# Operand sums on another engine, reordered steps, and split weights kept off chip in a three-stage transformer kernel

## The reference

```python
y = clip((x * styles) @ weight.T * dcoefs + bias)          # conditioned projection
h = rms_norm(y); gate = gelu(h @ Wg.T + bg); hs = h @ Wh.T + bh
r, i = sigmoid(h @ Wr.T + br), sigmoid(h @ Wi.T + bi)
a = exp(-8 * softplus(alpha) * r)
out = scan(o = a * o + sqrt(1 - a * a) * hs * i)           # over the sequence
hs2 = out * gate + y
h2 = rms_norm(hs2)
g2 = gelu(h2 @ mlp_gate_w.T + mlp_gate_b)                  # 512 -> 1536
f2 = h2 @ mlp_fc_w.T + mlp_fc_b                            # 512 -> 1536
x1 = x + (f2 * g2) @ out_w.T + out_b + hs2                 # 1536 -> 512
# third part: conditioned norms of x1, a 3072 -> 512 -> 512 MLP, an int8-quantised product, added to x1
```

## Time and profile before

| | |
|---|---|
| median of the runs | 1802.99 us |
| the profiled execution | 1807.12 us, its span 1805.0 us |
| TensorE busy | 1754.0 us (97%) |
| VectorE, ScalarE, GpSimd busy | 1191.8, 891.6, 833.2 us |
| scan half, about | 0 to 463 us |
| gate and fc stage, about | 463 to 957 us |
| output stage, about | 957 to 1264 us |
| third part | to 1805 us |

### The profile page before, as it was taken

How to read it: one execution, slowest core, us unless ns; L and a number is a source line. 1 busy time by engine, 2 the same in 40 slices (tenths; PEclk the granted TensorE clock), 3 DMA queues, 4 the chain that set the end, 5 groups by cost and what they waited for, 6 DMA issues and landing times.

```text
span 1805.0 us, 23628 instructions
## 1 busy us (share of the span) xinstructions
PE 1754.0 (97%) x8039; PEld 1424.1 (79%) x8047; DVE 1191.8 (66%) x1737; ACT 891.6 (49%) x1325; POOL 833.2 (46%) x718
## 2 busy tenths in 40 slices
PE   9999999999789999999999999898999999999998
PEld 7888888887578787887887888776888888888886
DVE  8766676659769779677564334445986776686555
ACT  7655555655456565565562222223554453544533
POOL 1112222123667667667660000014577777877743
PEclk9999999999889999999999999999999999999999
DMA  5011110010232433332445657786744345444411
GB/s 201 1 47 47 47 46 19 28 70 27 82 126 94 148 110 109 117 124 70 170 145 198 208 185 232 260 297 227 258 130 164 118 141 182 119 156 149 136 40 59
DMA packets 105789, 229.63 MB, mean 127 GB/s; under 512 B 9906, under 2 KB 10162, under 8 KB 105700
## 3 DMA queue, kind: packets, MB, share of 16 engines
q1 hardware_dynamic: 75540, 152.97, 24.9%
q0 software_dynamic: 11776, 41.95, 7.0%
q10 hardware_dynamic: 18384, 33.56, 5.7%
HBM read 169.73 MB, written 58.72 MB: 127 GB/s over the span
## 4 chain that ended last, share of the span: by engine, by line
PE 83%; DVE 7%; DMA 3%; issue 3%; ACT 2%; POOL 1%; SPq 1%; DVEq 0%; ACTq 0%; POOLq 0%
PE bank L1031 22%; PE bank L342 16%; PE bank L1967 13%; PE bank L1093 12%; PE bank L2012 5%; PE bank L1991 4%; PE bank L322 4%; PE bank L1933 2%; PE bank L1942 2%; DVE h_parts L1435 1%; DMA raw_w<-int_W 1%; DVE mlp_w L1444 1%; PE bank L1103 1%; SPq L1860 1%; DMA raw_mlp_w<-mlp_gate_g 0%
## 5 line engine op out<-in xcount | busy, mean ns | idle before, releaser
L1031 PE MATMUL bank<-h_parts,mlp_w 128*128 128x512 f32 x2016 | 467.8, 394 | 25.4 <-DVE mlp_w L1439 9.7
L1031 PEld LDWEIGHTS bank<-h_parts,mlp_w 128*128 128x128 f32 x2016 | 382.6, 190 | 110.0 <-DVE mlp_w L1439 11.8
L342 PE MATMUL bank<-h_parts,gate_w 128*128 128x512 f32 x1536 | 351.4, 389 | 1.8 <-ACT gelu_out L532 1.3
L342 PEld LDWEIGHTS bank<-h_parts,gate_w 128*128 128x128 f32 x1536 | 288.1, 188 | 63.5 <-ACT gelu_out L532 1.7
L1093 PE MATMUL bank<-p_parts,mlp_out_w 128*128 128x512 f32 x1152 | 274.6, 395 | 12.2 <-DVE p_parts L1449 10.7
L1967 PE MATMUL bank<-operand_parts,int_w 128*128 128x512 f32 x1152 | 281.8, 394 | 0.6 <-DVE x_columns L1528 0.6
L1093 PEld LDWEIGHTS bank<-p_parts,mlp_out_w 128*128 128x128 f32 x1152 | 215.2, 189 | 62.9 <-issue 15.8
L1967 PEld LDWEIGHTS bank<-operand_parts,int_w 128*128 128x128 f32 x1152 | 213.1, 188 | 44.6 <-PE bank L1093 1.0
L594 POOL TENSOR_TENSOR decay_sq<-decay 128x512 f32<-128x512 f32 x32 | 38.3, 1196 | 274.5 <-DVE decay L680 274.5
L1362 POOL TENSOR_TENSOR product_out<-product_out,gelu 128x512 f32<-128x512 f32 x72 | 126.6, 1780 | 69.2 <-DVE product_out L1498 68.7
L1240 ACT ACTIVATE product_copy<-bank,vec_sb 128x512 f32<-128x512 f32 x144 | 98.9, 689 | 97.2 <-PE bank L1031 97.0
(11 more groups left out here) (306 smaller groups left out, 2850.7 us busy)
## 6 DMA issues: line engine op xcount, KB each, us to landing
p_d<-product_out SPq DMA_DIRECT2D x96, 256.0 KB, 2.1
p_tile<-p_d ACTq DMA_DIRECT2D x96, 256.0 KB, 4.3
raw_mlp_w<-mlp_gate_g SPq DMA_DIRECT2D x21, 512.0 KB, 3.8
raw_mlp_w<-mlp_fc_g SPq DMA_DIRECT2D x21, 512.0 KB, 4.5
xin<-xT SPq DMA_DIRECT2D x8, 1024.0 KB
hs_d<-u SPq DMA_DIRECT2D x8, 1024.0 KB, 5.0
hs_pair<-hs_d SPq DMA_DIRECT2D x8, 1024.0 KB, 5.4
x_columns<-xT SPq DMA_DIRECT2D x8, 1024.0 KB, 6.8
```

What stands on the lines that cost most here:

```text
L342: i = pe.matmul(bank[:], gw[:, w, s, k, m * P:(m + 1) * P], hr[:, q, t, k, :], start=k == 0 and n == 0, stop=k == KT - 1 and n == 2)
L1031: i = pe.matmul(bank[:], wb[g % 2][:, s, w, kk, :], hop[u % 2][o][:, t, kk, :], start=first and kk == 0 and n == 0, stop=kk == 1 and n == ...
```

## The change

1. Only visits 0 to 5 (the first pair, `NPREP` = 6) load raw weights, form sums and split. After the split SyncE stores the whole buffer to DRAM (`keep_parts`, 1.8 MB per k and chunk). The later visits with a new chunk (15, `RELOADS`) fetch the parts back in two pieces (`parts_back`): part 0 is what products 1, 5 and 6 read, part 1 the rest; the layout of `wb` is turned so that each piece is contiguous.
2. The sums of the operands (T1 to T4) move from GpSimd to VectorE. The steps beside the groups are spread anew.
3. At the seam to the gate and fc stage: mean-square steps earlier, the fc weights of visit 0, T4 and group 0's copies and sums moved into the last block of the scan half.
4. At the seam to the output stage: the first three tiles are split one step earlier.
5. In blocks 5 and 6 of the output stage: the small tables and four of the six slots are asked for ahead of the x1 stores and their waits.

```diff
-A11, A12, A22, S1, S2, S3, S4 = range(NM)
+A11, S1, S2, A12, S3, S4, A22 = range(NM)
+PARTS = ((0, A12), (A12, NM))
-NPREP = len(CHUNK)
+NPREP = FT // 2
+RELOADS = [v for v in range(NPREP, NV) if NEW[v]]
...  scan half, ScalarE, body (the early(-3) ahead of the block is gone)
+                if not nxt2:
+                    early(4 if not nxt else -3)        # after the square roots
                 for m in range(KT):
+                    if m == 2 and not nxt:
+                        early(5)                       # between the gelus
...  scan half, VectorE, body
+                if not nxt:
+                    early(4)                           # before the scans
+                if not nxt:
+                    early(5)                           # after the scans
...  SyncE
+        def keep_parts(k, n):
+            sp.wait_ge(w_lo[k], 2 * (n + 1))
+            sp.dma_start(w_d[2 * CHUNK[n] + k], wb[k][:]...).then_inc(w_stored[k], 16)
+
+        def parts_back(k, i, part):
+            a, b = PARTS[part]
+            sp.wait_ge(w_stored[k], 16 * NPREP)
+            sp.wait_ge(p_ps[(6, 4)[part]], 2 * (i - 1) + k + 1)
+            sp.dma_start(wb[k][:, a:b]..., w_d[2 * VISITS[i][2] + k, :, 4 * P * a:4 * P * b]).then_inc(w_back[k][part], 16)
         def visit(i):
             if i == 0:
+                keep_parts(0, 0)
                 next_pair(1)
-            n = PREP[i] + 1
-            ahead = NEW[i] and n < NPREP
-            if ahead:
-                sp.wait_ge(w_sum[0], 4 * n)
-                sp.wait_ge(w_lo[0], 2 * n - 1)
-                load_raw(0, n)
+            n = i + 1
+            if i < NPREP:
+                keep_parts(1, i)
+                if n < NPREP:
+                    sp.wait_ge(w_sum[0], 4 * n)
+                    sp.wait_ge(w_lo[0], 2 * n - 1)
+                    load_raw(0, n)
+            if i in RELOADS:
+                parts_back(1, i, 1)
             if i:
                 sp.wait_ge(p_end, i)
                 store(i - 1, 3)
-            if ahead:
+            if n < NPREP:
                 sp.wait_ge(w_sum[1], 4 * n)
                 sp.wait_ge(w_lo[1], 2 * n - 1)
                 load_raw(1, n)
+                keep_parts(0, n)
+            if n in RELOADS:
+                parts_back(0, n, 0)
+                parts_back(0, n, 1)
+                parts_back(1, n, 0)
...  SyncE, output stage, body
+            if b == LAST_FIRST:
+                last_small()
+            if b == NB - 2:
+                last_slots()                           # slots 2 to 5
             if b:
                 sp.wait_ge(r1, KT * b)
...
-                last_small()
...
             if b == NB - 2:
-                last_slots()
+                last_late_slots()                      # slots 0 and 1
...  TensorE, group: waits for w_lo in visits 0 to 5, for w_back in RELOADS
+            weights_ready(g, 0)                        # before product 1
+            weights_ready(g, 1)                        # before product 3
...  ScalarE
         def weights_high(k, n):
             act.wait_ge(raw_loaded[k], 16 * (n + 1))
             if n:
+                act.wait_ge(p_ps[4], 2 * (n - 1) + k + 1)
+                act.wait_ge(w_stored[k], 16 * n)
-            if g == NG - 1:
+            if g == NG - 2:
                 for n in range(HEAD):
                     tile_high(n)
             elif m == 3:
+                weights_high(0, 0)
                 operand_high(0, T3)
                 operand_high(0, T2)
-                weights_high(0, 0)
                 weight_sums_high(0, 0)
+            elif m == 4:
+                weights_high(1, 0)
+                weight_sums_high(1, 0)
+                operand_high(0, T4)
+                copy_1(0)
+                copy_5(0)
+            elif m == 5:
+                copy_6(0)
...  GpSimd: operand_sums and its calls are gone
...  VectorE
+        def operand_sums(u, part):
+            t = tsum[u % 2]
+            if part == 0:
+                dve.wait_ge(h_full, 2 * KT * (u + 1))
+                dve.tensor_tensor(t[T1][:], half(1, 0), half(0, 0), ALU.subtract).then_inc(t_sum, 1)
+                dve.tensor_tensor(t[T3][:], half(1, 1), half(1, 0), ALU.subtract).then_inc(t_sum, 1)
+            else:
+                dve.tensor_tensor(t[T2][:], t[T3][:], half(0, 0), ALU.add).then_inc(t_sum, 1)
+                dve.tensor_tensor(t[T4][:], half(0, 1), t[T2][:], ALU.subtract).then_inc(t_sum, 1)
...  beside, steps: 4 invert 0; 5 normalise 0; 6 invert 1; 7 normalise 1, low B11; 8 sums T1, T3, low B21;
...  9 sums T2, T4, low B22; 10 low T1, T3, T2; 11 low T4 (before: 5 to 8 invert and normalise in turn;
...  9 low B11, B21, B22; 10 low T1, T3; 11 low T2, T4)
+            if g == NG - 1:                            # before sum_out(g, ...)
+                for n in range(HEAD):
+                    tile_low(n)
         def early(m):
             elif m == 2:
-                for o in (B11, B21, B22, T1):
-                    operand_low(0, o)
+                operand_low(0, B11)
+                operand_low(0, B21)
+                operand_sums(0, 0)
+                operand_sums(0, 1)
             elif m == 3:
-                operand_low(0, T3)
-                operand_low(0, T2)
+                operand_low(0, B22)
                 weights_low(0, 0)
                 weight_sums_low(0, 0)
+                for o in (T1, T3, T2):
+                    operand_low(0, o)
+            elif m == 4:
+                weights_low(1, 0)
+                weight_sums_low(1, 0)
+                operand_low(0, T4)
+            elif m == 5:
+                for t in range(3):
+                    sum_out(0, t)
```

More of the change, by code:

```diff
@@ L823, in mlp_half, with own, summed @@
     rstd = [at(f"rstd2_{n}", [P, BT], where) for n, where in enumerate(ROOT_AT)]
-    wb = [at(f"mlp_w{k}", [P, 2, NM, 2, P], WB_AT[k], F32R) for k in range(2)]
+    wb = [at(f"mlp_w{k}", [P, NM, 2, 2, P], WB_AT[k], F32R) for k in range(2)]
+    def own(k, s):
+        return wb[k][:, A11:NM:3, s]
+    def summed(k, s):
+        return wb[k][:, S1:NM, s].rearrange("p (a b) k o -> p a b k o", b=3)[:, :, 0:2]
     raw = [at(f"raw_mlp_w{k}", [P, 4, 2, P], RAW_AT[k]) for k in range(2)]
@@ L847, in mlp_half @@
     w_lo = (early_sem("mlp_gate_low"), early_sem("mlp_fc_low"))
+    w_stored = (early_sem("mlp_gate_parts_stored"), early_sem("mlp_fc_parts_stored"))
+    w_back = [[early_sem(f"mlp_{n}_parts_back{part}") for part in range(2)] for n in ("gate", "fc")]
     ow = [at(f"mlp_out_w{n}", [P, 2, KT, D], where, F32R) for n, where in enumerate((G2, F2, O2))]
@@ L1038, in last_product, with weights_ready @@
             product(g, 4, X[g % 2], False)
+        def weights_ready(g, part):
+            k, i = g % 2, g // 2
+            if i < NPREP:
+                pe.wait_ge(w_lo[k], 2 * i + 1)
+            elif i in RELOADS:
+                pe.wait_ge(w_back[k][part], 16 * (RELOADS.index(i) + 1))
         def group(g):
             k, i = g % 2, g // 2
-            n = PREP[i]
-            pe.wait_ge(w_lo[k], 2 * n + 1)
+            weights_ready(g, 0)
             if g == 0:
@@ L1053, in group @@
             product(g, 1, X[k], True)
-            pe.wait_ge(w_lo[k], 2 * n + 2)
+            if i < NPREP:
+                pe.wait_ge(w_lo[k], 2 * i + 2)
             if g > 1:
@@ L1501, in group @@
             beside(g)
-            if g % 2 == 0 and g:
+            if g == NG - 1:
+                for n in range(HEAD):
+                    tile_low(n)
+            if g == 0:
+                return
+            if g % 2 == 0:
                 product_21(g // 2 - 1)
@@ L1510, in group @@
             sum_out(g, 2)
-            if g == 0:
-                operand_low(0, T4)
-            if g == NG - 1:
-                for n in range(HEAD):
-                    tile_low(n)
         def add_hs2(b, ks):
@@ L1544, in early @@
                 add_squares(0, 0)
+            elif m == -3:
+                add_squares(0, 1)
             elif m == -1:
-                add_squares(0, 1)
                 sum_low(0, 0)
@@ L1882, in run @@
                 sp.wait_ge(stored[t], 16 * NB)
-        return early_small, early_w1, early_c_rows, early_w2, early_slots, early, run
+        return early_small, early_w1, early_c_rows, early_w2, early_slots, late_slots, early, run
     def tensor_program(pe, mlp, bank_at):
```

169 lines of the change are left out of this document (83 added, 86 removed).

## The result

The changed kernel took 1818.26 us (median of four runs, 1817.50 to 1818.74) against 1804.11 (four runs, 1802.51 to 1806.01) of the kernel before on the same chip: ratio 1.0078, 95% interval 1.0060 to 1.0095. It is slower, by 14.1 us; 1814.3 was forecast. The profiled execution took 1818.66 us, its span 1816.9.

A forecast was written before the change was run, and what follows sets the result against it. TensorE was taken to bound the block-pair products, so only its holes could be won; +9.5 + 19 - 5.5 - 1.4 - 8.2 - 2.1 = +11.3 us on the median 1803.0 gave 1814.3 us, range 1782 to 1829.

The forecast's parts named there:

- The seam: From scan half to gate and fc stage: two 1.835 MB stores ahead of the raw weights delay TensorE, +9.5 us.
- The first visits: First six visits: raw gate loads wait behind fc split and store; losses 3.7, 3.7, 5.7, 7.2, taken as +19 us.
- Visits 6 to 23: Later gate and fc visits: nothing is split, so holes of pairs 2 and 3 go, -5.5 us; fetches cost nothing.
- a fetch that TensorE waits for: Sign of a wrong forecast, in the later visits; fetches 1 us late each visit would cost +15 us.
- The output stage: Low tiles split earlier -1.4 us, small tables asked for sooner -8.2, four slot loads moved ahead -2.1.
- the joint: Entry to the output stage: HEAD's low tiles ahead of the last sum remove the 1.43 us hole, -1.4 us.
- what is late next: Output stage, after the small tables come sooner: the x columns' load, for which VectorE waited 5.10 us without a hole.
- the next bound: Output stage: VectorE's mixed_w work, named with bounds of -5 to +5 us around the x1T store's count of nothing.
- the stores hide: Rival for seam and visits: loads behind the stores land as before; -24 us, 1779 us, chance 0.15.
- The slipping loop: Rival: GpSimd's multiply and SyncE's product stores pace the first visits (+27), with clock loss at holes; 1827 us, chance 0.17.
- Half hidden: Rival: seam as forecast, but the first visits lose only 1 to 2 us each, 6 in all; 1801 us, chance 0.17.

The follow-up runs named there:

- seam_early: The changed kernel with chunk 1's raw weights loaded and chunk 0's parts stored in the last scan block, ahead of the store of u; 1798.94 us.
- raw_first: The changed kernel with the raw gate load ahead of the store of the fc parts from visit 1 on, seam as it is; 1800.36 us.
- no_keep: The changed kernel without its stores and fetches of parts: all 21 chunks loaded raw and split; 1784.96 us.
- no_keep_gpsimd_sums: no_keep with the operand sums T1 to T4 back on GpSimd at the same steps; 1792.87 us.
- output_loads_only: The kernel before with only the change's order of small-table and slot loads in the output stage; 1798.25 us.
- both_orders: The changed kernel with the edits of seam_early and raw_first together; 1782.12 us.
- no_keep_early_2: no_keep with chunk 1's raw weights asked for in the last scan block, ahead of the store of u, run a second time; 1775.51 us.

## Why the prediction was right, and where it was not

**The seam: right in kind, the term too large.** Forecast +9.5, measured +4.8 with the start-up apart. One hole of over 20 us, ended by ScalarE's copy, stands where it was put, and TensorE returns 1.47 us after the landing (before 1.48). From the store of u to the landing it was 13.07 us before and is 20.84 now: the two stores cost 7.8 us, not 9.5. 3.67 MB at the 385 GB/s of this stretch are 9.5 us, but the queue before was not full all the time (321 GB/s from 487.58 to 500.65), and the stores took some of its empty room. The rest of the difference is the store of u, 3.0 us earlier by the scan half's own time, which the text had left in place "within 2 us either way". The Trainium skill (DMA: Bandwidth & Descriptors, Queues, rings and completion order) has each DMA engine consume a ring's descriptors in order; seam_early and raw_first agree, the place of the same transfers alone is worth 19.3 and 17.9 us.

The prediction left two holes of before out of its account (2.42 and 0.58). What it priced at nothing there, the earlier arrival of TensorE, proved so in the change: it arrived 9.3 us sooner (484.60 against 493.88) and only waited longer. But the move of the sums is worth 4.8 us at this point in no_keep against no_keep_gpsimd_sums, with both waiting 15 us for the DMA: it makes the store of u earlier, and through it all that stands behind it. The prediction looked only at TensorE's arrival.

**The first visits: right in all, not turn by turn.** Forecast 20.3, taken as 19, measured 20.9. From SyncE's release at 522.14 to the landing at 530.10 it was 8.0 us where 9.3 was worked out; from landing to product 5, 6.2 where 6.1 was. Of the terms, the four turns have holes of 2.57, 2.91, 5.49 and 4.49 us against 3.7, 3.7, 5.7 and 7.2. The 5.4 us that the holes do not explain lie in TensorE itself. Behind the hole of 4.23 us, 48 matmuls took 13.18 us, 2.3 more than at 0.2272 each, with the granted clock at 0.63 (third row of the stretches). The 72 at 559.35 took 1.1 more, the 36 at 595.45 took 0.7 more, and four other runs that end at a hole 0.3 each, as before (six in 1.66 instead of 1.36). For these visits the text had a clock loss only in one rival. It also had product 7 add nothing of its own, since it comes ready with product 5. Product 7's holes come first at each turn and make 9.55 of the 15.46 us; at the third turn, 581.01, product 7 waits 4.23 us and product 5 behind it not at all. All four turns lost less by holes than was worked out, and TensorE's slower runs filled the sum: that part is luck. That VectorE's later steps lengthen these turns was an estimate, and no run tests it.

**Visits 6 to 23: the size right, the reason wrong.** Forecast -5.5, measured -4.9 (less the 0.63 at 915.13, the late fetch behind the output weights: it had been placed 1 us before its need, and a fetch that TensorE waits for was named as a sign of being wrong, here a small one). But the reason given was that "nothing is split", and from it followed that the holes of group 11 stay; they fell from 2.86 to 0.43 us. no_keep splits everything and has none of these holes: the step that failed is the attribution. The new spread of the beside steps takes them away by itself, so they cannot be credited to the stores and fetches, which pay for nothing. That is why undoing them gains 33 us.

**The output stage: too hopeful.** Forecast -11.7 for its three parts, measured -7.8; the joint gave its 1.4. The four holes of before, 5.59, 2.10, 0.66 and 2.37 us, became 1.37, none, 1.05 and 2.13, and 0.81 and 0.16 are new: 5.2 us less. The clock loss of 2.6 behind the 5.59 went, and one of 1.4 came behind the 2.13 (12 matmuls in 4.38 us). TensorE waits for VectorE's p_parts each time, and at the first two VectorE itself had stood waiting for the load of the x columns:

```profile
1174.27 1.41 DVE L1586 SCALAR_TENSOR_TENSOR x_columns<-hs_odd,vec_sb,x_columns 128x512 f32<-128x512 f32 x2 [5.10 <-DMA x_columns<-xT]
1175.60 2.47 DVE L2629 BATCH_NORM_STATS2 stats<-x_tiles 128x6 f32<-128x512 f32 x4
...
1218.45 1.41 DVE L1586 SCALAR_TENSOR_TENSOR x_columns<-hs_even,vec_sb,x_columns 128x512 f32<-128x512 f32 x2 [10.65 <-DMA x_columns<-xT]
```

So "what is late next" was named rightly, the load of the x columns; that it makes no hole was the mistake. Ahead of 1179.57 the third part's statistics (2.47 us) stand behind the same wait of 5.10 that made no hole a block earlier. At the second, the wait of before was 6.96 (1203.19) and made no hole; the load is asked for at the same time after the stage's first product (235.6 us, before 235.9), VectorE now comes to it 6.7 us sooner while it lands 3.0 sooner (both from that first product), and the wait is 10.65. output_loads_only shows the same two waits, 5.15 and 10.57, in the kernel before with this order alone. At the last two VectorE is busy with the third part's steps, mixed_w among them, which the text had named as the next bound.

**The sum.** 4.8 + 20.9 - 2.4 - 4.9 - 7.8 makes +10.6 against +11.3: the seam's excess and the output stage's shortfall cancelled, so the closeness is luck in part. The forecast was 4.0 us low at the end: its base, 1803.0, lies 1.1 below the median of the comparison, and the medians differ by 14.1 where 11.3 was counted. Added to the profiled 1807.1, for which it had been worked out, it would have been 1818.4. Start-up scatter of up to 3.8 us between executions means neither base is clean.

**The rivals.** That the stores hide is refuted by the landing at 506.93. The slipping loop did not come in full: the first visits lost 21 us, not 27, and its low clock came once, for 2.3 us. Half hidden did not come either: the first visits lost all that was worked out.

**Open:** the last 4 to 5 us hole at the seam; 1.3 of the 6.6 us between both_orders and no_keep_early_2, which are not idle time of this stage's products; the 2.7 us that the move of the sums is worth behind the seam; how much of the gain at the seam each of the steps moved there brings.

## What to carry to other kernels

A bulk store can cost little by its bytes and much by its place: put loads that a near step waits for ahead of it in the queue, here 36 us of 1818 for the same traffic, against 6.6 for storing and fetching at all instead of splitting again. Before paying for stored results, test whether the repeated work costs any time at all; here the split of the later pairs was free once its steps were spread. When an edit makes an engine earlier ahead of a wait, follow it also to the DMA that the same engine releases.

## What the runs showed of the hardware

- The queue of one core moved 385 GB/s over 20 us of mixed stores and loads with all engines still, about the 388 of the earlier trace rows.
- TensorE's granted clock fell to 0.63 behind a hole of 4.23 us and to 0.50 behind 23.80 us, but behind 2.79 us (607.12) 12 matmuls took 3.01 us, at the full clock (1.00); behind 2.80 us in seam_early (585.75) 12 took 4.44. The hole of 2.13 us near 1267 came with slow matmuls in the change and at full clock in no_keep (12 in 2.96 at 1235.45), and so did that of 2.37 in the kernel before (12 in 3.00). The length of the hole alone does not tell.
- VectorE and GpSimd slowed each other in two-operand operations like these. The change ran T1 and T3 on VectorE in 1.21 us each with GpSimd idle and three subtractions of the same size in 5.11 us beside GpSimd's sums; of GpSimd's 128x256 sums the same lines took 1.45 and 1.72 us there and 0.74 and 0.73 with VectorE nearly idle:

```profile
449.19 1.21 DVE L1475 TENSOR_TENSOR h_sum<-hs_pair 128x1024 f32<-128x1024 f32 x1
...
461.51 5.11 DVE L1492 TENSOR_TENSOR h_parts<-h_sum,h_parts 128x1024 fp32r<-128x1024 f32 x3
```
```profile
459.06 1.45 POOL L1402 TENSOR_TENSOR mlp_w_sums<-raw_mlp_w 128x256 f32<-128x256 f32 x1
```
```profile
483.86 0.74 POOL L1378 TENSOR_TENSOR mlp_w_sums<-raw_mlp_w 128x256 f32<-128x256 f32 x1
```

The first two fences are of the change, the last of no_keep_early_2. The three sums that follow it took 0.73, 0.73 and 0.72 us.
